# A decoder layer whose order of work is a table of times: own times for every job, three buffers for the dense experts, two of three adds on POOL

## What is computed

```
x = layernorm(x + FAVOR attention(x))     # 16 heads of 64, 128 random features, causal, linear
x = layernorm(x + cross attention(x))     # 77 context rows, 32 half heads, differential softmax
x = layernorm(x + MoE(x))                 # 16 experts of 128, top 4 (2 of 4 groups), and a shared expert
```

```
qp = exp(q @ W - |q|^2 / 2); kp = exp(k @ W - |k|^2 / 2)
S_t = S_(t-1) + k_t v_t;  y_t = (q_t S_t) / (q_t z_t + eps);  out = y @ Wo
y = sum over the 4 chosen experts of weight * (silu(x g_e) * (x u_e)) d_e,  plus the shared expert
```

## Time and profile before

| | us |
|---|---|
| runs | 994.81, 997.05, 1001.26 (median 997.05) |
| profiled execution | 1003.07, span 1001.3 |
| PE busy | 844.2 (84%) |
| DVE busy | 667.8 (67%) |
| ACT, POOL busy | 497.0, 346.1 |
| mean granted clock of TensorE | 0.921 |

### The profile page before, as it was taken

One profiled execution on the slowest core, in us unless ns is written; L12 is line 12 of the kernel. 1 busy time (PEld: TensorE's weight loads), 2 busy tenths in 40 slices (PEclk: granted clock), 3 DMA queues, 4 the chain that ended last, 5 costly groups with the idle time before them and its releaser, 6 DMA issues.

```text
span 1001.3 us, 19630 instructions
## 1 busy us (share of the span) xinstructions
PE 844.2 (84%) x6908; PEld 627.8 (63%) x6908; DVE 667.8 (67%) x1714; ACT 497.0 (50%) x1003; POOL 346.1 (35%) x376
## 2 busy tenths in 40 slices
PE   5899978998898899899989989986497876699763
PEld 2578756866676687667768767775275664575331
DVE  4577734457777765777875576877385667664888
ACT  4777744443775443468553437720146753454221
POOL 5211100100583143139415215913314662355121
PEclk9999977999999999999999999997688998799985
DMA  8366565411121133101123221243432322323341
GB/s 297 96 166 172 136 123 139 120 49 50 38 50 52 55 97 87 41 22 31 46 75 107 80 80 32 80 175 129 153 101 91 91 88 71 98 93 113 116 153 72
DMA packets 70158, 96.65 MB, mean 97 GB/s; under 512 B 19632, under 2 KB 50480, under 8 KB 69552
## 3 DMA queue, kind: packets, MB, share of 16 engines
q1 hardware_dynamic: 63408, 78.87, 28.1%
q0 software_dynamic: 5376, 15.47, 4.2%
q10 hardware_dynamic: 1280, 1.05, 0.4%
HBM read 42.33 MB, written 33.10 MB: 75 GB/s over the span
## 4 chain that ended last, share of the span: by engine, by line
PE 49%; DVE 27%; ACT 8%; issue 6%; SPq 5%; DMA 3%; POOL 2%; ACTq 0%; DVEq 0%
PE ps L1517 23%; PE ps L1614 4%; PE ps L1617 4%; PE ps L1595 4%; SPq L692 3%; PE ps L1604 3%; DVE xmax L1378 2%; PE ps L1585 2%; PE ps L1586 2%; PE ps L1587 2%; PE ps L1574 2%; PE ps L1672 1%; DVE low_parts L1323 1%; DVE st L1188 1%; DVE yT L1497 1%
## 5 line engine op out<-in xcount | busy, mean ns | idle before, releaser
L883 POOL TENSOR_TENSOR low_parts<-square,qk 128x512 f16<-128x512 f32 x64 | 76.0, 1187 | 407.4 <-DVE qk L1325 407.3
L1323 DVE SCALAR_TENSOR_TENSOR low_parts<-ps,qk 128x512 f16<-128x512 f32 x64 | 44.1, 689 | 113.8 <-ACT square L974 109.2
L890 POOL TENSOR_TENSOR prob<-prob_full,prob 128x512 f16<-128x512 f32 x84 | 99.3, 1201 | 7.6 <-ACT prob_full L1018 6.2
L912 POOL DMA_INDIRECT rows_out<-attn_mem,dest x64 | 61.8, 966 | 111.2 <-ACT attn_mem L1069 97.5
L1517 PE MATMUL ps<-x_split,w_qkv 128*128 128x512 f16 x384 | 99.3, 397 | 0.9 <-DVE low_parts L1323 0.9
L969 ACT ACTIVATE qk<-ps 128x512 f16<-128x512 f32 x64 | 38.2, 596 | 118.9 <-PE ps L1517 113.4
L1614 PE MATMUL ps<-attn_mem 128*128 128x65 f32 x512 | 93.6, 276 | 2.7 <-issue 2.1
L1614 PEld LDWEIGHTS ps<-attn_mem 128*128 128x128 f32 x512 | 81.0, 197 | 10.8 <-issue 3.1
L1617 PE MATMUL ps<-run,attn_mem 128*128 128x65 f32 x384 | 76.5, 282 | 0.0
L985 ACT ACTIVATE attn_mem<-ps 128x512 f32<-128x512 f32 x64 | 38.5, 602 | 75.6 <-PE ps L1587 74.8
L1595 PE MATMUL ps<-attn_mem 128*128 128x128 f32 x512 | 72.4, 286 | 2.8 <-issue 2.8
(11 more groups left out here) (284 smaller groups left out, 2137.6 us busy)
## 6 DMA issues: line engine op xcount, KB each, us to landing
qk<-low_parts SPq DMA_DIRECT2D x128, 128.0 KB, 2.4
attn_mem<-rows_in SPq DMA_DIRECT2D x64, 144.0 KB, 2.4
late_mem<-ffn_w SPq DMA_DIRECT2D x17, 384.0 KB, 3.8
rows_in<-zero_row SPq DMA_DIRECT2D x32, 144.0 KB, 2.2
up_split<-late_mem SPq DMA_DIRECT2D x16, 256.0 KB, 3.3
x_stage<-xT SPq DMA_DIRECT2D x4, 512.0 KB, 4.4
down_split<-late_mem SPq DMA_DIRECT2D x16, 128.0 KB, 3.6
rows<-x SPq DMA_DIRECT2D x4, 512.0 KB, 4.6
```

Of the source, the lines that this page charges most:

```text
L883: pool.tensor_tensor(low_parts[:, n % 2, 1, :], square[:, n % 2, :], qk[:, n % 2, n // 2 % 2, 0, 1, :], ALU.subtract).then_inc(p_sql.sem, 1)
L890: pool.tensor_tensor(prob[:, n % RING, 1, :], prob_full[:, n % FULL, :], prob[:, n % RING, 0, :], ALU.subtract).then_inc(pr_low.sem, 1)
L912: pool.indirect_dma_start(rows_out[b], bass.IndirectOffsetOnAxis(ap=dest[:, i % YB, j:j + 1], axis=0), yb[:, i % YB, j, :], None).then_inc ...
L1323: dve.scalar_tensor_tensor(low_parts[:, n % 2, 0, :], bank[:, :], 1 / W_SCALE, pair[:, 0, 0, :], ALU.mult, ALU.subtract).then_inc(p_low.se ...
```

## The change

Three edits.

1. Every kind of job has its own time in steps (tables ATT, CHAIN, END), and schedule() sorts the jobs by time. In a head step "k features" now follows "q features", then "attend", "state", "turn output", "output" (they were: state, attend, turn output, k features, output). The jobs of a chain keep about their places, but "queries" follow "turn stream" at once, "probs" start about half a step earlier, "turn cross" and "gate" have other jobs between them, and "route" 1 to 3 are later. In the end a step is now tile down, tile up, tile turn, with "turn maxima" ahead of a step and "probs" behind it, a step between "turn cross" and "gate", and two between "route" 3 and "weights".
2. dense_h and dense_hT have three buffers (DR = 3) and take all of prob_mem; wT moves to xv.
3. In "combine" POOL does the first two adds; DVE waits for them and does the third.

```diff
+ATT = dict(project=-1.94, turn_keys=1.1, q_features=0.2, values_0=0.17, values_1=0.17, state=2.57, attend=1.45,
+           turn_output=5.6, k_features=0.36, output=3.73)
...
+END = dict(out=-3.81, out_d=1.205, norm1=-0.18, turn=-0.17, queries=-0.16, scores=1.04, scores_d=0.211, maxima=8.72,
+           probs=9.4, probs_d=0.247, norm2=17.99, cross=19.47, gate=20.35, route0=20.52, up=21.03, route1=21.52,
+           route2=21.84, down=22.52, route3=21.85, weights=23.04, dense=23.67, dense_d=2.109, dense_2=1.323,
+           pick=0.65, keep=2.0, sum=4.75, sums=37.0, sums_d=1.0, sums_n=0.77)
...
-        dense_h = prob_mem[:, 0:1024].rearrange("p (r t) -> p r t", r=2)
+        dense_h = prob_mem[:, 0:1536].rearrange("p (r t) -> p r t", r=DR)
...
+                elif kind == "combine":
+                    i = NT * b + n
+                    four = yg[i % YG]
+                    pool.wait_ge(*yg_loaded[i % YG](i // YG + 1, 0))
+                    pool.tensor_tensor(four[:, 0:2, :], four[:, 0:2, :], four[:, 2:4, :], ALU.add).then_inc(paired.sem, 1)
+                    pool.wait_ge(*paired(i, 1))
+                    pool.tensor_tensor(four[:, 0, :], four[:, 0, :], four[:, 1, :], ALU.add).then_inc(paired.sem, 1)
...
-                    if n >= 2:
-                        act.wait_ge(*dn_low(0, n - 1))
+                    if n >= DR:
+                        act.wait_ge(*dn_low(0, n - DR + 1))
...
-                    dve.wait_ge(*yg_loaded[i % YG](i // YG + 1, 0))
+                    dve.wait_ge(*paired(i + 1, 0))
                     four = yg[i % YG]
-                    link(dve.tensor_tensor(four[:, 0:2, :], four[:, 0:2, :], four[:, 2:4, :], ALU.add))
-                    link(dve.tensor_tensor(four[:, 0, :], four[:, 0, :], four[:, 1, :], ALU.add))
                     dve.tensor_tensor(total[:, n, :], four[:, 0, :], total[:, n, :], ALU.add).then_inc(folded.sem, 1)
```

More of the change, by code:

```diff
@@ L73 @@
 XG, YB, YG = 8, 3, 3
+DR = 3
 WROW = 32
 UP, DOWN = 2, 4
-def attention_jobs(t):
-    jobs = []
-    def add(kind, g, per):
-        if 0 <= g < NBLK * per:
-            jobs.append((kind, g // per, g % per))
-    if t + 2 >= 2:
-        add("project", t + 2, H)
-    add("turn keys", t - 1, H)
-    add("q features", t, H)
-    add("state", t - 2, H)
-    add("attend", t - 1, H)
-    if t % 2 == 1:
-        add("turn output", (t - 5) // 2, PAIRS)
-    add("k features", t, H)
-    add("output", t - 3, H)
-    for b in range(1, NBLK):
-        for c in range(NT):
-            if t == H * b - NT + c:
-                jobs.insert(3, ("values", b, 2 * c))
-            if t == H * b + NT - 1 + c:
-                jobs.insert(3, ("values", b, 2 * c + 1))
-    return jobs
@@ new lines @@
+ATT = dict(project=-1.94, turn_keys=1.1, q_features=0.2, values_0=0.17, values_1=0.17, state=2.57, attend=1.45,
+           turn_output=5.6, k_features=0.36, output=3.73)
+CHAIN = dict(out=4.28, out_d=0.239, norm1=5.03, turn=5.55, queries=5.56, scores=6.82, scores_d=0.071, maxima=9.36,
+             probs=9.86, probs_d=0.165, norm2=14.72, cross=15.45, gate=15.84, route0=15.97, up=16.24, route1=17.71,
+             route2=18.29, down=18.08, route3=19.1, prefix=19.61, dispatch=19.62, keep=19.63, ends=20.45)
@@ new lines, in chain_jobs @@
+def chain_jobs(put, start, b, at):
+    for n in range(NT):
+        put(start + at["out"] + n * at["out_d"], "project out", b, n)
+    put(start + at["norm1"], "norm1", b, 0)
+    for n in range(2):
+        put(start + at["turn"], "turn stream", b, n)
+    for n in range(KD):
+        put(start + at["queries"], "queries", b, n)
+    for n in range(NT * NG):
+        put(start + at["scores"] + n * at["scores_d"], "scores", b, n)
+    put(start + at["maxima"], "turn maxima", b, 0)
+    for n in range(CHUNKS + LAG):
+        when = start + at["probs"] + n * at["probs_d"]
+        if n < CHUNKS:
+            put(when, "probs", b, n)
+        if n >= LAG:
+            for _, _, m in weighs(b, n - LAG):
+                put(when, "weigh", b, m)
+    put(start + at["norm2"], "norm2", b, 0)
+    for n in range(2):
+        put(start + at["cross"], "turn cross", b, n)
+        put(start + at["up"], "shared up", b, n)
+        put(start + at["down"], "shared down", b, n)
+    put(start + at["gate"], "gate", b, 0)
+    for n in range(4):
+        put(start + at[f"route{n}"], "route", b, n)
+    if b == DENSE:
+        put(start + at["weights"], "weights", b, 0)
+    else:
+        put(start + at["prefix"], "prefix", b, 0)
+        put(start + at["dispatch"], "dispatch", b, 0)
+        put(start + at["keep"], "keep", b, 0)
+        if b == GROUPS[GROUP_OF[b]][-1]:
+            put(start + at["ends"], "ends", GROUP_OF[b], 0)
+            put(start + at["ends"], "table", GROUP_OF[b], 0)
@@ L224, in schedule @@
     first = [(bb, c) for bb in GROUPS[0] for c in range(NT)]
-    ahead = [[] for _ in range(len(first) + 2)]
     for i, (bb, c) in enumerate(first):
-        ahead[i].append(("fetch", bb, c))
-        ahead[i + 2].append(("combine", bb, c))
+        put(END["sums"] + i * END["sums_d"], "fetch", bb, c)
+        put(END["sums"] + (i + 2) * END["sums_d"], "combine", bb, c)
         if c == NT - 1:
-            ahead[i + 2].append(("norm3", bb, 0))
-    rest = [job for part in dense[done:] for job in part]
@@ L232, in schedule @@
-    jobs += merged(rest, [job for part in ahead for job in part])
-    jobs += [("total", DENSE, c) for c in range(NT)] + [("norm3", DENSE, 0)]
-    return jobs
-def dense_jobs(e):
-    jobs = []
-    for kind, k in (("dense gate", e), ("dense up", e), ("dense weigh", e - 1), ("dense keep", e - 1),
-                    ("dense down", e - 2)):
-        if 0 <= k < NE:
-            jobs.append((kind, DENSE, k))
-    return jobs
+            put(END["sums"] + (i + 2) * END["sums_d"] + END["sums_n"], "norm3", bb, 0)
```

176 lines of the change are left out of this document (68 added, 108 removed).

## The result

| | before | after |
|---|---|---|
| time, us (median of the runs timed together) | 998.28 (994.81 to 1001.26) | 937.67 (935.64 to 940.16) |
| ratio, 95% interval | | 0.9395 [0.9354, 0.9436] |
| span of the profiled execution | 1001.3 | 933.9 |
| mean granted clock of TensorE | 0.921 | 0.966 |

The kernel is 60 us faster, where 42 were forecast. Timed again beside other kernels, the same program gave 0.9369 [0.9332, 0.9405].

What follows compares the result with a forecast made beforehand. PE was taken to bound the heads, PE with waits the tiles, DVE the tail. Tail -20, tiles -10, clock -3 and heads -9 made -42, from the median 997.05 to 955 us; range 930 to 982.

Steps and rivals of the forecast that it cites:

- the second rival: Whole kernel: nearly all named waits go and the clock stays up; tail -24, tiles and clock -30, heads -20: 923 us; chance 0.13.
- Heads, -9 forecast: Heads of the blocks: 15 us of PE waits filled, 3 lost at queries, 3 at k features; bounds +8 to -22.
- the 3 of the queries: Heads: queries follow turn stream with nothing between, so PE waits 1 us more a block, 3 us.
- the 3 of the k features: Block 0 heads: k features come 0.5 to 1 us too early for 6 or so heads, costing 3 us.
- Tiles and clock, -13 forecast: Tiles: 13 us of PE waits filled, 3 given back for DVE's queue, so -10; fewer clock falls, -3.
- the 3 for the clock: Tiles: PE waits less, so its clock falls less often; at most 8.6 us could be won, 3 taken.
- Tail, -20 forecast: Tail: two adds to POOL and three buffers leave DVE 42.4 us, so 63 us become 42 to 43; bounds -25 to -5.
- I cost these waits at nothing: Tail: with three buffers DVE's waits for tanh, such as 2.62 us at 922.56, were taken as hidden by other work.
- The third rival: Tail: POOL becomes the bound through slow adds, held-up adds and a longer tanh ring; tail gives -5, 970 us; chance 0.10.
- The first (only the tail gains): Heads and tiles: the new order trades one wait for another, only the tail's 20 us are won: 977 us; chance 0.18.
- The fourth (early k features stall all blocks): Heads: early k features stall PE at every second head in all blocks; at 2 us each, 1028 us; chance 0.05.
- The last sentence of the prediction: Whole kernel: the frame is wrong if PE's waits shrink but stretches don't, as its busy time would hide slow issue.

Runs made afterwards that it cites:

- the first four experiments: Kernel before with: three buffers and POOL adds (1.0088); POOL adds alone (1.0083); new order inside head steps (0.9963); new heads and chains, old end (0.9709).
- the four experiments behind them: Old heads with new end (0.9683); changed kernel with old order inside head steps (0.9510), two buffers (0.9413), or all adds on DVE (0.9499).

## Why the prediction was 17 us too high

The measured 60 us lie in the stated range, but outside the band that the forecast gave itself (-30 to -55); the range had been stretched half way to the second rival.

**Heads, -9 forecast, -29 measured: the step that failed.** The count of waits nearly held. From 180.02 to 639.15 before and from 175.40 to 606.92 after, between the same two key projections, PE's idle time falls from 33.4 to 17.5 us, 15.9 less. Of the forecast, 15 less the 3 of the queries belong here, so 12; the 3 of the k features lie in block 0. The waits of 2.14, 2.05 and 3.75 us of the earlier trace rows stand at 1.31 for the probs of block 2 and under 1 us for the others, and between the heads no wait over 1 us is left but the queries and that one. The two costs held as well. The queries wait 1.72, 1.73 and 3.07 us, 2.6 us more in all than before (3 forecast). The k features of block 0 wait 8.5 us for their moved low parts where they had waited 3.7, 4.8 more (3 forecast), and this is the order's own cost: 7.3 to 8.8 us in the eight profiles with the new order inside a step, 3.5 to 3.7 in the six with the old one; in block 1 two such waits stand in both kernels (10.1 before, 9.4 after), in blocks 2 and 3 none.

What was left out is that a wait costs more than it shows. In the same stretch PE's busy time falls by 11.7 us (425.74 to 414.06), with the clock from 0.97 to 1.00: 27.3 us of it were at 1.2 GHz, and 3.4 are. The sum gave the tiles a term for the clock and the heads none, although had 0.96, 0.97 and 0.99 for them: 0.04 x 180 + 0.03 x 180 + 0.01 x 120 = 13.8 us of full-speed work that was lost, which is close to what came back. The stretch is 27.6 us shorter in all; another 4.6 us are won ahead of it. There the first four heads of block 1 stand at 0.75 to 0.85 before and only the third, at 0.78, after. But profiles of the same order differ by more than 4.6 us there (block 1 took 162.7 to 168.3 us in five of them, block 2 161.5 to 161.6), so the cause of these is open. In the traces the miss of the heads is then 11.7 us for the busy time, 3.9 for more waits gone than counted, and 7.6 ahead of 175 us, where 4.6 were won and 3 were to be lost.

**Tiles and clock, -13 forecast, -19.2 measured.** By waits of the earlier trace rows: probs 5.02 to 1.41 (3 forecast to go, 3.6 went), gate 6.71 to 0.90 (4, 5.8), weights 8.17 to 4.67 (5, 3.5), cross 2.80 to 1.23 (1, 1.6), the probs behind POOL 3.44 to 1.99 (0, 1.5). That is 16.0 where 13 was counted; the 3 us given back for a crowded DVE did not come. The weights' 4.67 is over the 3 us named ahead as a sign. Busy time fell by 2.2 us, for 3 forecast. The mechanism was right and a little undersized, but the 3 for the clock came near by luck, for its working was wrong. The clock has two levels here: in before it reads 0.50 from 349.0 to 352.0 and 1.00 from 352.5. So a mean of 0.91 says that 0.18 of the 191 us were at half speed, 34 us, and 17 us of full-speed work were lost; the prediction took 17 for the first and 8.6 for the second. In the tail it did the same (12 us, not 6). That much was not to be had either: from 0.91 to 0.96 the share times the stretch is 11 us, and the busy time fell by 2.2. Part of the low clock falls on PE's waits, as from 758.4 to 763.0 before, at 0.50 with 2.48 of 4.60 us busy; the rest is not explained.

**Tail, -20 forecast, -14.0 measured.** Two sizes were wrong, in opposite directions. DVE lost 15.5 us of busy time (50.05 to 34.51), where 10.6 was counted: the third adds are 0.92 us each and not 1.26 (10.17 us for 11, against 9.67 for as many before), since POOL's adds cover only part of them; and 2.2 us are in other instructions of DVE. But "I cost these waits at nothing" failed. DVE is idle 10.6 of 45.1 us, as it had been 9.0 of 59.0. The waits for tanh were read in the earlier trace rows as the ring of two buffers; the third buffer is worth 2.0 us, and two of these waits are ACT's queue behind norm3. The row shown at 922.56 was of the ring, the two later in the tail, at 948.71 and 971.83 with the same 2.62 us, were not, and I had taken one for all. ACT's timeline of before has the tanh of the first behind POOL's subtraction, and that of the second behind norm3's scalings (L1088):

```profile
921.93 0.60 ACT L1079 ACTIVATE prob<-ps 128x512 f32<-128x512 f32 x1 [1.33 <-POOL prob L917]
...
946.13 2.07 ACT L1088 ACTIVATE yT<-yT,shift,rstd 128x256 f32<-128x256 f32 x4 [2.66 <-DVE shift L1506]
948.11 0.57 ACT L1079 ACTIVATE prob<-ps 128x512 f32<-128x512 f32 x1
```

POOL's pair takes 1.27 + 0.75 = 2.0 us, near the 1.8 taken from the larger add; the bound of 3.2 was far off. The third rival's mechanism, adds on POOL that hold up the tail, is not a question of their price: with the same prices it decides in the old order (1.0088) and is absent in the new one. That edit 3 hangs on the place of the pair, and that edit 2 gives nothing in the old order (a tail of 67.64 us with either number of buffers), was not in the prediction, which summed the parts as if each could stand alone.

**The rivals.** The first (only the tail gains) is out: heads and tiles give most. The fourth (early k features stall all blocks) is out: no such wait in blocks 2 and 3. The second, everything named goes and the clock stays up (923 us), was as near as the forecast, 15 us below the result where that was 17 above: the clock between the heads came out as it says, the tail did not.

**The last sentence of the prediction,** that the frame is wrong if busy time hides something, was the right doubt with the wrong sign: waits shrank by what was counted, and the stretches shrank by more.

## What to carry to other kernels

Where PE bounds a stretch, count what its waits cost at the clock as well: if the granted clock of a stretch is below 1.00, the share below it times the stretch can be had beside the idle time, once the waits ahead of the fall are filled. Between the heads, with PE busy over 92%, this gave 13.8 us where 11.7 came; among the tiles, with PE busy 81%, it gives 11 where 2.2 came, so there it is a bound and no more. Before work is moved to another engine, look at what stands ahead of it in that engine's order and at what the receiver has queued behind its own wait; here that place decided between 9 us lost and 10 us won, at nearly the same price of the instructions. When two waits in a profile have the same length, follow each back before one explanation is used for both.

## What the runs showed of the hardware

**A DVE cast with one input is held up by POOL too.** The longer wait of block 3 at the queries (3.08 against 1.73 us) starts in DVE's timeline, where a cast (L1300) takes 1.49 us beside POOL's 1.17 us at 528.77, and 0.41 us in block 2:

```profile
366.47 0.41 DVE L1300 CAST qk<-square 128x512 f16<-128x512 f32 x1
528.74 1.49 DVE L1300 CAST qk<-square 128x512 f16<-128x512 f32 x1
```

In the five profiles with the new heads in which this cast takes 1.49 or 1.50 us and the queries stand where they do in after, PE waits 3.04 to 3.11 us; in the one with the old end, in which no such cast is held up, it waits 1.73. So 1.1 us of a held-up cast became 2.7 us of a head, through the clock.

The Trainium skill (SBUF — State Buffer, SBUF: two separate sides) names, beside DVE operations with two SBUF inputs, those in a two-port performance mode as the ones that exclude GpSimd. Whether this cast runs in such a mode, no run here shows.

**In the first four experiments the dispatch slows PE.** In the set with 1042.95 us, the heads in which POOL issues its scattered rows take 29.7 to 31.7 us in blocks 2 and 3, in all four kernels, against 18.1 for the same 150 matmuls in all others. One of them, with one of PE's waits in it:

```profile
357.58:388.47 30.89, 23.28 (x150) 16.42 (x149) 7.90 (x25) 4.55 (x8) 14.07 (x15) 0.78 0.27 92
...
372.86 0.37 PE L1518 MATMUL ps<-w_o,yT 128*128 128x256 f16 x1 [1.73 <-issue]
```

PE waits there for nothing that the trace shows, and DVE and ACT are nearly idle as well. These two heads make up 25 to 26 of the 43 us; about 20 more fall between the last head and the tail. What holds them was not tried and stays open. Nor is it shown to belong to the chip: the four experiments behind them are on record with the same chip number, and there the kernel before takes 1000.21 us. It is in every kernel of the set, so the ratios there are of a longer total.
